# Reciprocals of attention denominators spread through DRAM instead of by TensorE, with new orders on all engines

## The reference

```python
q, k, v = xn @ Wq + bq, xn @ Wk + bk, xn @ Wv + bv      # 16 heads of 64
Q, K = elu(q) + 1.0, elu(k) + 1.0
KV = einsum('bshd,bshm->bhdm', K, v)
Z = 1.0 / (einsum('bshd,bhd->bsh', Q, K.sum(axis=1)) + EPS)
o = einsum('bshd,bhdm,bsh->bshm', Q, KV, Z)
x = layer_norm(xn + o @ Wo + bo, g1, be1)
s = layer_norm(x + gelu(x @ W1 + b1) @ W2 + b2, g2, be2)
h = silu(fp4_linear(xn, w_gate)) * fp4_linear(xn, w_up)
out = src + s * silu(fp4_linear(h, w_down))
```

## Time and profile before

| | |
|---|---|
| Median of 3 runs | 1667.33 us (1667.31 to 1667.33) |
| The profiled execution | 1668.97 us, span of the core 1667.2 us |
| TensorE clock granted | 0.998 of full speed |
| PE busy | 98% of the span |
| DVE busy | 78% |
| ACT busy | 59% |
| POOL busy | 47% |
| DMA queues | 16% of 16 engines |

### The profile page before, as it was taken

How to read it: one execution, slowest core, us unless ns; L and a number is a source line. 1 busy time by engine, 2 the same in 40 slices (tenths; PEclk the granted TensorE clock), 3 DMA queues, 4 the chain that set the end, 5 groups by cost and what they waited for, 6 DMA issues and landing times.

```text
span 1667.2 us, 30550 instructions
## 1 busy us (share of the span) xinstructions
PE 1640.6 (98%) x11105; PEld 1467.2 (88%) x11105; DVE 1300.8 (78%) x2571; ACT 978.6 (59%) x1770; POOL 784.1 (47%) x750
## 2 busy tenths in 40 slices
PE   7999999999999999999999999999999999999997
PEld 6878888888899998989999999989899999999897
DVE  6685664555879797888879897979787887979796
ACT  6665666655464656565655656465656565564644
POOL 4564443434234445444453535444544446353447
PEclk9999999999999999999999999999999999999999
DMA  7322323331300101021010102010101111010100
...
DMA packets 69987, 89.36 MB, mean 54 GB/s; under 512 B 8384, under 2 KB 54604, under 8 KB 68815
## 3 DMA queue, kind: packets, MB, share of 16 engines
...
## 4 chain that ended last, share of the span: by engine, by line
PE 69%; DVE 2%; POOL 1%; ACT 0%; issue 0%; POOLq 0%; DVEq 0%
PE QH L81 7%; PE AC L81 7%; PE AC L83 7%; PE AC L82 7%; PE QH L83 7%; PE QH L82 7%; PE GU L81 5%; PE GU L83 5%; PE GU L82 5%; PE TT L821 3%; PE QH L715 2%; PE DN L700 2%; PE DN L81 2%; PE DN L82 2%; PE DN L83 2%; DVE x L1860 1%
## 5 line engine op out<-in xcount | busy, mean ns | idle before, releaser
L1217 ACT ACTIVATE rh<-QH 128x512 fp32r<-128x512 f32 x256 | 149.2, 597 | 82.5 <-DVE QH L1933 77.7
L81 PE MATMUL GU<-wgh,xqh 128*128 128x352 f32 x512 | 169.8, 332 | 0.9 <-DVE hb L1768 0.4
L82 PE MATMUL GU<-wgl,xqh 128*128 128x352 f32 x512 | 165.1, 322 | 0.0
L83 PE MATMUL GU<-wgh,xql 128*128 128x352 f32 x512 | 165.0, 322 | 0.0
L2428 POOL TENSOR_TENSOR hb<-hb,rs_h 128x704 f32<-128x704 f32 x64 | 89.0, 1391 | 158.0 <-DVE rs_h L1775 158.0
L1264 ACT ACTIVATE hb<-GU 128x352 f32<-128x352 f32 x128 | 59.4, 464 | 175.5 <-PE GU L83 173.8
L1948 DVE TENSOR_TENSOR rl<-QH,rh 128x512 fp32r<-128x512 f32 x128 | 86.9, 689 | 87.0 <-ACT rh L1217 85.7
L81 PE MATMUL AC<-Mh,rh 128*128 128x256 f32 x512 | 145.7, 285 | 0.1
L81 PE MATMUL AC<-w2h,rh 128*128 128x256 f32 x512 | 144.5, 282 | 0.0
L82 PE MATMUL AC<-w2l,rh 128*128 128x256 f32 x512 | 142.8, 279 | 0.0
L83 PE MATMUL AC<-w2h,rl 128*128 128x256 f32 x512 | 142.8, 279 | 0.0
...
## 6 DMA issues: line engine op xcount, KB each, us to landing
...
xt_scratch<-xth SPq DMA_DIRECT2D x32, 256.0 KB, 2.8
xt_scratch<-xtl SPq DMA_DIRECT2D x32, 256.0 KB, 3.0
...
xnTh<-xt_scratch SPq DMA_DIRECT2D x32, 256.0 KB, 4.7
xnTl<-xt_scratch SPq DMA_DIRECT2D x32, 256.0 KB, 5.4
...
m_scratch<-mh SPq DMA_DIRECT2D x16, 256.0 KB, 2.4
```

The lines of the kernel that those rows point to most:

```text
L81: e.matmul(outp, lh, rh, start=start, stop=False, skip_group_check=check)
L82: e.matmul(outp, lh, rl, start=False, stop=False, skip_group_check=check)
L83: return e.matmul(outp, ll, rh, start=False, stop=stop, skip_group_check=check)
L1217: e.activation(RH[j % 4][:], src, ACT.Copy).then_inc(S[sem], 1)
```

## The change

- `z_spread`, `z_parts`, the tiles `zhi`, `zd`, `sel` and their set-up on DVE are gone. `den_inverse` is the sum and the reciprocal alone.
- SP's `z_out(g)` stores the 16 useful rows of each tile to DRAM with four DMAs; `z_in(g, j)` loads the row of a head to 64 partitions with one DMA, two for each `j`, into a ring of four tiles `ZB`. It waits for all four stores of its group and, through `zq`, for the multiplication that frees its tile. They stand on SP's list ahead of the loads for the next group.
- `z_mul` multiplies `Q32[:, j]` in place by `ZB`, both in SBUF; `z_hi` reads SBUF.
- `z_lo` moves from DVE to POOL and reads SBUF.
- `q_elu` of the next group waits for `z_hi` and `z_lo` in place of `z_mul`. `turn_x1` no longer waits for them.
- The lists of PE, ACT, DVE and POOL are in another order. On PE, `f_step(g - 1, 4..7)` come later, two of them and two `down` between `den_sums(g)` and `at_step(g, 0)`.

```diff
+            def z_out(g):
+                w.wait_ge(S["zi"], 2 * g + 2)
+                for t in range(4):
+                    e.dma_start(z_dram[g, :, t * 128:(t + 1) * 128], dn_s[32 * t:32 * t + 16, :]).then_inc(S["zo"], 16)
+
+            def z_in(g, j):
+                w.wait_ge(S["zo"], 64 * (g + 1))
+                w.wait_ge(S["zq"], 8 * g + j - 3)
+                for s in range(2):
+                    e.dma_start(ZB[j % 4][64 * s:64 * s + 64, :],
+                                z_dram[g, 2 * j + s].unsqueeze(0).broadcast_to([64, 512])).then_inc(S[f"zb{j % 4}"], 16)
...
             for g in range(NG):
+                z_out(g)
+                for j in range(8):
+                    z_in(g, j)
                 if g + 1 < NG:
                     load_xb(g + 1)
                     load_xn(g + 1)
...
-                e.matmul(QH[:, (j % 2) * 512:(j % 2 + 1) * 512], sel[:, j, :], zd[:], start=True, stop=True).then_inc(S["zs"], 1)
...
             def z_mul(g, j):
-                bank = QH[:, (j % 2) * 512:(j % 2 + 1) * 512]
-                w.wait_ge(S["zs"], 8 * g + j + 1)
+                w.wait_ge(S[f"zb{j % 4}"], 32 * (2 * g + j // 4 + 1))
+                w.wait_ge(S["Q"], 8 * g + j + 1)
                 w.wait_ge(S["dn"], g + 1)
-                e.tensor_tensor(bank, Q32[:, j, :], bank, ALU.mult).then_inc(S["zq"], 1)
+                e.tensor_tensor(Q32[:, j, :], Q32[:, j, :], ZB[j % 4][:], ALU.mult).then_inc(S["zq"], 1)
...
+            def z_lo(g, j):
+                w.wait_ge(S["zq"], 8 * g + j + 1)
+                w.wait_ge(S["zh"], 8 * g + j + 1)
...
+                e.tensor_tensor(RL[j % 4][:], Q32[:, j, :], f(RH[j % 4][:]), ALU.subtract).then_inc(S["zl"], 1)
```

The new list of PE from `den_sums` to the end of the attention steps (b, c, d are tiles of group g, the marks - 4 of the group before):

```diff
+                den_sums(g)
+                gate_up(b, 0)
+                turn_h(d - 4, 0)
+                down(c - 4)
+                gate_up(b, 1)
+                turn_h(d - 4, 1)
+                f_step(g - 1, 6)
+                f_step(g - 1, 7)
+                down(d - 4)
+                turn_xq(g, 1)
+                at_step(g, 0)
+                at_step(g, 1)
+                at_step(g, 2)
+                at_step(g, 3)
+                gate_up(c, 1)
+                turn_h(a, 0)
+                at_step(g, 4)
+                at_step(g, 5)
+                turn_h(a, 1)
+                at_step(g, 6)
+                at_step(g, 7)
```

In group 0 only `gate_up(1, 0)`, `gate_up(1, 1)` and `turn_xq(0, 1)` stand between `den_sums(0)` and `at_step(0, 0)`. DVE's and POOL's new lists around the step:

```diff
+                den_inverse(g)
+                h_scale(a)
+                gate_mul(b, 0)
+                x_round(g, 1)
+                h_lo(d - 4, 0)
+                h_round(a)
+                h_lo(d - 4, 1)
+                g_mul(c - 4)
+                z_mul(g, 0)
+                z_mul(g, 1)
+                ln_add("lnb", g - 1, 0)
+                ln_add("lnb", g - 1, 1)
+                z_mul(g, 2)
+                z_mul(g, 3)
...
+                z_lo(g, 0)
+                z_lo(g, 1)
+                z_lo(g, 2)
+                z_lo(g, 3)
+                h_out(a)
+                z_lo(g, 4)
+                z_lo(g, 5)
+                h_in(b)
+                z_lo(g, 6)
+                z_lo(g, 7)
```

More of the change, by code:

```diff
@@ new lines, in _ @@
+            down(NT - 6)
+            gate_up(NT - 3, 1)
+            turn_h(NT - 5, 1)
+            f_step(NG - 2, 6)
+            f_step(NG - 2, 7)
+            down(NT - 5)
+            turn_xq(NG - 1, 1)
+            at_step(NG - 1, 0)
+            at_step(NG - 1, 1)
+            at_step(NG - 1, 2)
+            at_step(NG - 1, 3)
+            gate_up(NT - 2, 1)
+            turn_h(NT - 4, 0)
+            at_step(NG - 1, 4)
+            at_step(NG - 1, 5)
+            turn_h(NT - 4, 1)
+            at_step(NG - 1, 6)
@@ new lines, in _ @@
+            at_step(NG - 1, 7)
+            gate_up(NT - 2, 0)
+            turn_h(NT - 3, 0)
+            down(NT - 4)
+            turn_x1(NG - 1, 0)
+            turn_x1(NG - 1, 1)
+            gate_up(NT - 1, 0)
+            h_proj(NG - 1, 0)
+            h_proj(NG - 1, 1)
+            turn_h(NT - 3, 1)
+            gate_up(NT - 1, 1)
+            h_proj(NG - 1, 2)
+            h_proj(NG - 1, 3)
+            f_step(NG - 1, 0)
+            h_proj(NG - 1, 4)
+            f_step(NG - 1, 1)
+            h_proj(NG - 1, 5)
@@ L2113, in _ @@
             kv_out(NB - 1, 1)
+            x_round(0, 0)
             q_elu(0, 2)
@@ new lines, in _ @@
+                gelu_lo(g - 1, 5)
+                gelu_lo(g - 1, 6)
+                g_mul(a - 4)
+                gelu_lo(g - 1, 7)
+                h_round(d - 4)
+                x_scale(g, 0)
+                q_elu(g, 0)
+                q_elu(g, 1)
+                h_lo(c - 4, 0)
+                x_round(g, 0)
+                x_max(g, 1)
+                h_lo(c - 4, 1)
+                q_elu(g, 2)
+                q_elu(g, 3)
+                x_scale(g, 1)
+                xq_lo(g, 0)
+                q_elu(g, 4)
@@ new lines, in _ @@
+                ln_add("lnb", g - 1, 0)
+                ln_add("lnb", g - 1, 1)
+                z_mul(g, 2)
+                z_mul(g, 3)
+                gate_mul(b, 1)
+                xq_lo(g, 1)
+                h_max(b)
+                z_mul(g, 4)
+                z_mul(g, 5)
+                z_mul(g, 6)
+                h_scale(b)
+                z_mul(g, 7)
+                ln_stats("lnb", g - 1)
+                h_lo(a, 0)
+                gate_mul(c, 1)
+                h_round(b)
+                h_lo(a, 1)
@@ new lines, in _ @@
+                gate_mul(d, 1)
+                h_lo(b, 1)
+                gelu_lo(g, 2)
+                h_max(d)
+                gelu_lo(g, 3)
+                h_round(c)
+                gelu_lo(g, 4)
+                h_scale(d)
+                x_max(g + 1, 0)
+            gelu_lo(NG - 2, 5)
+            gelu_lo(NG - 2, 6)
+            g_mul(NT - 8)
+            gelu_lo(NG - 2, 7)
+            h_round(NT - 5)
+            x_scale(NG - 1, 0)
+            q_elu(NG - 1, 0)
+            q_elu(NG - 1, 1)
@@ new lines, in _ @@
+            h_lo(NT - 6, 0)
+            x_round(NG - 1, 0)
+            x_max(NG - 1, 1)
+            h_lo(NT - 6, 1)
+            q_elu(NG - 1, 2)
+            q_elu(NG - 1, 3)
+            x_scale(NG - 1, 1)
+            xq_lo(NG - 1, 0)
+            q_elu(NG - 1, 4)
+            q_elu(NG - 1, 5)
+            gate_mul(NT - 4, 1)
+            q_elu(NG - 1, 6)
+            q_elu(NG - 1, 7)
+            g_mul(NT - 7)
+            gate_mul(NT - 4, 0)
+            h_max(NT - 4)
+            den_inverse(NG - 1)
@@ new lines, in _ @@
+            h_scale(NT - 4)
+            gate_mul(NT - 3, 0)
+            x_round(NG - 1, 1)
+            h_lo(NT - 5, 0)
+            h_round(NT - 4)
+            h_lo(NT - 5, 1)
+            g_mul(NT - 6)
+            z_mul(NG - 1, 0)
+            z_mul(NG - 1, 1)
+            ln_add("lnb", NG - 2, 0)
+            ln_add("lnb", NG - 2, 1)
+            z_mul(NG - 1, 2)
+            z_mul(NG - 1, 3)
+            gate_mul(NT - 3, 1)
+            xq_lo(NG - 1, 1)
+            h_max(NT - 3)
+            z_mul(NG - 1, 4)
@@ new lines, in _ @@
+            z_mul(NG - 1, 5)
+            z_mul(NG - 1, 6)
+            h_scale(NT - 3)
+            z_mul(NG - 1, 7)
+            ln_stats("lnb", NG - 2)
+            h_lo(NT - 4, 0)
+            gate_mul(NT - 2, 1)
+            h_round(NT - 3)
+            h_lo(NT - 4, 1)
+            ln1_add(NG - 1, 0)
+            ln1_stats(NG - 1, 0)
+            g_mul(NT - 5)
+            ln1_add(NG - 1, 1)
+            ln1_stats(NG - 1, 1)
+            gate_mul(NT - 2, 0)
+            ln1_norm(NG - 1)
+            xT_half(NG - 1, 0, "x1T", "x1Th", "x1Tl")
@@ L2649, in _ @@
+            ln1_rstd(NG - 1, 1)
+            x2_affine(NG - 2)
+            final_mul(NG - 2)
+            final_add(NG - 2)
+            h_in(NT - 2)
+            h_out(NT - 2)
+            h_in(NT - 1)
             last_scale(0)
```

907 lines of the change are left out of this document (329 added, 578 removed).

## The result

The changed kernel takes 1749.09 us (median of 4 runs, 1744.99 to 1750.64), the kernel before 1667.33 beside it: a ratio of 1.0484, 95% interval 1.0463 to 1.0504. I had forecast 1650, faster; it is 82 us slower, and outside the range. The page of after, to be set beside the earlier trace rows: busy times, chain, and the groups of the low part, of an attention step's first product and of `z_mul` (xcount | busy us, mean ns | idle before it and its releasers).

What follows compares the result with a forecast made beforehand. PE was taken as the bound. A group gains 2.4 - 0.25 - 0.75 = 1.4 us, 15 groups 21.0; less 2.5 and 0.8 that is 17.7 off 1667.3, so 1650 us, range 1632 to 1676.

Steps and rivals of the forecast that it cites:

- What bounds the kernel: Whole kernel: PE, busy 98% of the span and 77.03 of a 77.22 us period, sets the time.
- Part 1: PE's eight spreads a group go away: 2.4 us a group gained, bounds 1.9 to 2.6.
- Part 2: Reciprocals through DRAM: load 2.4 us, store 2.0; at_step(g, 0) is met 0.5 us before PE's 11.7, no loss.
- Part 3: Low parts on POOL: its serial piece overhangs PE's arrival at at_step(g, 6) by 0.4 us; 0.25 a group taken.
- Part of it is won back: POOL's 0.4 us overhang shrinks to 0.25, since the next stop, turn_x1, already waits today.
- Part 4: DVE's z_mul and POOL both on SBUF: overlaps cost POOL 0.75 us a group, bounds 0 and 1.8.
- rival B: DVE and POOL: nothing new stalls, DVE has 12 us of slack a group; 32.7 us gained, 1635 us; chance 0.22.
- Part 5: Ends and order: group 0 costs 2.5 us, the end 0.8; new order nothing, bounds -0.5 to +0.5 a group.
- C: POOL beside DVE pays the full bound, 1.8 in place of 0.75 us a group: 1666 us, no change; chance 0.13.

Runs made afterwards that it cites:

- e13: e6 with x1_residual(g) moved on POOL's list from between h_in(c) and h_out(c) to behind h_in(d): 1668.5 us, ratio 1.0008.
- e3: The changed kernel with z_mul's second operand read from PSUM (not the reciprocals, so only its time counts): 1689.9 us, ratio 1.0129.
- e6: The changed kernel with both e3's PSUM operand for z_mul and e5's odd layout of am_h: 1688.8 us, ratio 1.0130.
- e5: The changed kernel with am_h in the odd layout, 11 rows of 4 columns with a gap, for h_scale's short operations: 1742.8 us, ratio 1.0453.
- e14: e5 with x1_residual(g) moved on POOL's list to behind h_in(d), the whole computation kept: 1713.4 us, ratio 1.0278.
- e8: The changed kernel, group 0 reordered: z_mul(0, 0) to (0, 3) ahead of h_round(0), z_lo(0, 0) and (0, 1) ahead of x_plus_bo(0): 1750.4 us.
- e11: The changed kernel with 8 fill products on PE ahead of turn_h(a, 1) and 8 ahead of at_step(g, 6), groups 1 to 14: 1738.6 us, ratio 1.0421.
- e15: e13 with POOL's h_in(b) moved behind z_lo(g, 7) as well: 1679.6 us, ratio 1.0073.

## Why the prediction was wrong, point by point

**What bounds the kernel.** Right for before; but that PE sets the time of after was an assumption of the sum.

**Part 1, the spreads: right.** e13 has a period of 76.36 us and one wait of 1.42 in it (the step before `at_step(g, 6)` takes 1.77 us in place of 0.35). Without it 74.9, and 77.2 less my 2.4 is 74.8. No run reached this period; it is a difference.

**Part 2, the DRAM way: right.** `z_mul(g, 0)` started 8.8 us after `den_sums` (I had 8.5) and `at_step(g, 0)` at 11.8 (11.7). A load landed in 3.0 us (2.4), a store in 1.4 (2.0):

```profile
DMA to landing us min/median/max: 2.6/3.0/4.1
...
z_scratch<-dn_s SPq DMA_DIRECT2D x64, 8.0 KB, 1.4
```

That the two errors cancel is luck. DVE waited only 2.5 us for the loads in all.

**Part 3, POOL's piece: right in kind, too small.** I had an overhang of 0.4 and took 0.25. Without `z_mul`'s contention the wait was 0.8 us in e3, where the piece ended at 23.4 (23.2 by my sum), and 1.4 in e6 and e13. The 0.6 between them is contention that I had not counted: low parts 6 and 7 took 3.17 us together in e6 in place of the 2.55 of my sum (2.58 in e3), with `h_round(b)` beside them on DVE. "Part of it is won back" did not happen.

**Part 4, two engines on SBUF: the step that failed.** I took 0.75 us a group, with 1.8 as the bound; e3 measures 4.0. Three errors. I priced the overlap as a slowing of POOL alone (0.26 us of an instruction, from a median in the earlier trace rows), while the runs show waiting on both sides: the one that comes second stands until the first ends. The row with 2273 ns in the earlier trace rows was such a wait: POOL's instruction began at 28.94 beside a DVE multiplication that ran from 28.30 to 30.06, and ended 1.2 us after it. I used it for the bound only. The other direction stood in the trace of before as well, a DVE operation on 44 columns beside a POOL instruction from 935.64 to 938.04:

```profile
935.65 2.44 DVE L1773 TENSOR_SCALAR am_h<-sn_h 128x44 f32<-128x44 f32 x1
```

I counted only meetings with `z_mul`, not those with `h_scale` and `h_round`, which the change also put beside a busy POOL: the earlier trace rows had the first instruction of `h_round` at 0.93 in the mean, after has (min/median/max)

```profile
L1753 DVE SCALAR_TENSOR_TENSOR hb<-hc,hb x64: 878/1635/3115, 446.7 to 1724.8; 128x704 f32<-128x704 f32 x64
```

And "DVE has 12 us of slack a group" (rival B) was taken over the whole period, while in the 14 us between `z_mul(g, 0)` and `at_step(g, 6)` POOL had 13.4 us of instructions (8 x 1.29 + 1.7 + 1.4) and DVE 5.4 us of `z_mul` (8 x 0.67) that could not lie beside them: 18.8 us in a stretch of 14, and `at_step(g, 6)` came 3.8 us late (26.6 against 22.8). Most of that sum could be made from rows of before. The Trainium skill states the rule that I needed on its page SBUF — State Buffer, Who interferes with whom: whoever starts first holds the pair of SBUF ports that DVE and POOL share for its whole instruction and the other is blocked; this concerns DVE's two-port modes, and its instructions with two SBUF inputs beside one of POOL that reads SBUF. I had cited only the line of GPSIMD Engine Reference that names the contention, without its kind. The runs agree with the rule at each point tested: `z_mul` with two SBUF inputs waits (up to 1.88 us), with one of them in PSUM it does not (673 ns), nor does the low part of GELU, which reads PSUM (673 to 694 ns in after); a reciprocal never waits (427 to 430 ns), and the short operation stops waiting once its two views have 11 rows and 44 columns.

**Part 5, the order at nothing: wrong by its neglect of POOL.** I looked at the new lists for the room that PE's steps leave and set bounds of 0.5 us a group. `h_round(c)` beside `x1_residual` cost 1.4 us a group (e6 against e13), and 2.5 in the unchanged computation (e5 against e14). The half microsecond of bounds had no term for POOL at all. In group 0 `at_step(0, 0)` started 15.7 us after `den_sums`, not 11.5, held by the order on DVE and POOL (e8). Its period lost 5.9 us, 1.1 more than the others, and the end 3.1 more than a group's loss, where I had 2.5 and 0.8.

**The clock was missing.** The sum has no term for it, as if the 0.998 of before stayed; after had 0.980. Behind PE's two waits of 1.2 us comes a dip to 1.2 GHz; by e11 it costs 0.9 us a group, which lie within the 4.0 of Part 4.

**The rivals.** None named the mechanism. C had it in kind but with 1.8 as its end. The balance of a period, from after down: 81.97 less 4.0 (the operand of `z_mul`, e3), 0.2 (short operations, e6), 1.4 (`h_round(c)` beside `x1_residual`, e13) and 1.4 (POOL's piece, its wait in e13) is 75.0, against 74.8 by Part 1. The last term is a wait read off and not one taken away: e15 removed it and lost more elsewhere. The odd layout lengthened POOL's piece by 0.6 us: they are part of the last term, and the second one is smaller by as much.
